# A vision tower's last stage on one core: scores, maximum and exponential run one tile further ahead of the transposes, with two probability buffers, ScalarE copying the attention output out of PSUM, and three gather buffers in place of four

## The reference

```python
# B=4, SEQ=2048, D=64, HEADS=8, KEYS=64, TOPK=16
x    = layernorm(h)
sim  = scores of x against two sets of 64 product keys     # per token, per head
rows = the 16 best of the 64 x 64 key pairs                # top-k of the sums
w    = softmax(the 16 best sums)
k, v = sum over the 16 rows of w * table[row]              # 128 values a token
q    = x @ Wq / 8
p    = softmax(causal(q @ k.T))                            # 2048 x 2048, masked
h   += (p @ v) @ Wo
```

## Time and profile before

| | |
|---|---|
| median of 3 runs | 13776.14 us (13771.75 to 13789.44) |
| profiled execution, first to last instruction | 17300.9 us; no other time of it is given |
| instructions | 137100 |
| TensorE matmuls busy | 10525.5 us (61%) |
| VectorE busy | 9604.5 us (56%) |
| ScalarE busy | 6663.5 us (39%) |
| GpSimd busy | 6947.2 us (40%) |

### The profile page before, as it was taken

The page is one execution under the profiler, slowest core; times in us unless marked ns, Lnnn a source line. Parts: engine busy times, 40 slices in busy tenths (PEclk is TensorE's granted clock), DMA queues, the critical chain, the costliest instruction groups (busy, mean ns, idle before and its releaser), DMA issues.

```text
span 17300.9 us, 137100 instructions
## 1 busy us (share of the span) xinstructions
PE 10525.5 (61%) x38012; PEld 5367.1 (31%) x38012; DVE 9604.5 (56%) x22115; ACT 6663.5 (39%) x13997; POOL 6947.2 (40%) x5868
## 2 busy tenths in 40 slices
PE   1564555554655366666666666666666666666667
PEld 1341222222212123333333333333333333333334
DVE  3327888887675654555544555455554454555542
ACT  0113333341002144444444444444444444444443
POOL 2004666764000254444444444444444444444442
PEclk9556777776677577877787778787877777777776
DMA  0001222221000111111111111111111111111110
GB/s 20 0 13 69 90 105 102 107 89 69 12 11 5 31 40 38 35 41 35 40 34 38 37 38 38 35 38 37 38 35 41 33 41 34 38 38 37 38 35 20
DMA packets 538556, 722.95 MB, mean 42 GB/s; under 512 B 412866, under 2 KB 420593, under 8 KB 503386
## 3 DMA queue, kind: packets, MB, share of 16 engines
q0 software_dynamic: 168448, 338.54, 7.4%
q1 hardware_dynamic: 369418, 376.55, 7.1%
HBM read 697.87 MB, written 8.42 MB: 41 GB/s over the span
## 4 chain that ended last, share of the span: by engine, by line
PE 25%; another core or an unknown queue 16%; ACT 14%; issue 7%; DVE 3%; DVEq 1%; ACTq 0%
ACT l3m_spread L2479 5%; PE l3m_O L2353 5%; PE l3m_acc L2385 4%; PE l3m_DX L2375 4%; PE l3m_S L2336 3%; ACT l3m_V L2521 2%; PE l3m_T L2343 2%; ACT l3m_prob L2508 2%; PE l3m_S L2375 2%; ACT l3m_W L2525 2%; ACT l3m_probT L2517 1%; PE l3m_DX L2376 1%; PE l3m_T L2296 1%; PE l3m_T L2321 1%
## 5 line engine op out<-in xcount | busy, mean ns | idle before, releaser
L2278 POOL DMA_INDIRECT l3m_got<-in_l_table,l3m_row x5120 | 4995.9, 976 | 6236.5 <-ACT l3m_spread L2479 3620.8
L2385 PE MATMUL l3m_acc<-l3m_W,l3m_values 128*128 128x512 f32 x3072 | 2014.8, 743 | 922.9 <-issue 512.8
L2734 DVE SCALAR_TENSOR_TENSOR tower_h<-l3m_O,l3m_pinv,tower_h 128x64 f32<-128x64 f32 x512 | 145.4, 284 | 3520.3 <-PE l3m_O L2353 2621.6
L2479 ACT ACTIVATE l3m_spread<-l3m_got,l3m_weight 128x128 f32<-128x128 f32 x5120 | 1924.1, 493 | 12.4 <-issue 12.4
L2517 ACT ACTIVATE l3m_probT<-l3m_T 128x512 f32<-128x512 f32 (+3 forms) x1280 | 679.8, 531 | 1756.8 <-remote 1108.3
L2353 PE MATMUL l3m_O<-l3m_vo_g,l3m_probT 128*128 128x64 f32 x5440 | 861.0, 306 | 678.5 <-ACT l3m_probT L2517 459.5
L1262 POOL TENSOR_TENSOR m_mul<-m_st,m_wide_c 128x2048 f32<-128x2048 f32 x256 | 1157.5, 4521 | 149.9 <-DVE m_st L1415 143.7
L2353 PEld LDWEIGHTS l3m_O<-l3m_vo_g,l3m_probT 128*128 128x128 f32 x5440 | 832.3, 222 | 916.2 <-ACT l3m_probT L2517 570.5
L2525 ACT ACTIVATE l3m_W<-l3m_DX 128x512 f32<-128x512 f32 x971 | 579.3, 597 | 1258.9 <-PE l3m_DX L2376 563.2
L2343 PE MATMUL l3m_T<-tower_ident,l3m_prob 128*128 128x128 f32 x4352 | 844.9, 317 | 286.9 <-issue 160.2
L2385 PEld LDWEIGHTS l3m_acc<-l3m_W,l3m_values 128*128 128x128 f32 x3072 | 592.9, 223 | 1301.5 <-issue 684.5
(11 more groups left out here) (689 smaller groups left out, 21609.8 us busy)
## 6 DMA issues: line engine op xcount, KB each, us to landing
m_wide_c<-l1a_c SPq DMA_DIRECT2D x256, 1024.0 KB, 4.6
l3m_got<-in_l_table,l3m_row POOLq DMA_INDIRECT x5120
l3m_values<-in_l_table SPq DMA_DIRECT2D x288, 256.0 KB
l0i_img<-in_l_x SPq DMA_DIRECT2D x4, 1024.0 KB, 7.9
l2r_x<-l2a_hT SPq DMA_DIRECT2D x8, 512.0 KB, 5.5
qp_inw<-in_q_inw SPq DMA_DIRECT2D x1, 2336.0 KB, 7.8
l_kept<-l0t_xt,l0t_row POOLq DMA_INDIRECT x128
l1a_c<-m_mul SPq DMA_DIRECT2D x16, 128.0 KB, 2.6
```

Source lines behind the costliest of these rows:

```text
L2278: pool.indirect_dma_start(got[:, unit % GOT, j, :], None, table, bass.IndirectOffsetOnAxis(ap=row[:, unit // QUAD % RING, unit % QUAD, j:j ...
L2385: pe.matmul(acc[:], values[:, tile, :], W[:], start=(tile == 0), stop=(tile == TILES - 1)).then_inc(blended, 1)
L2479: copy = act.activation(spread[:, unit % 2, :, j], got[:, unit % GOT, j, :], ACT.Copy, scale=weight[:, g % RING, t, j:j + 1])
```

## The change

TensorE's `scores` moves from the start of a step to its end and takes the tile after the next: at the end of step s it scores tile n + 2. VectorE's `peak` takes tile n + 1 in step s, and ScalarE's `attend` takes tile n + 1 in the middle of step s (behind turn `turns // 2`, and ahead of the `lift` of the next turn). For that `prob` has two buffers. `O` keeps one region of 64 columns; a new ScalarE copy `take_mix` at the start of each step brings tile n - 1's output to `mixes` (four slots), and `scale` reads it there one step later than before. The extras q, kv and vo are made three tiles ahead in place of two, `GOT` falls from 4 to 3, and there is one step more.

```diff
-STEPS = QUAD * (QUADS + LAG) + 1
+STEPS = QUAD * (QUADS + LAG) + 2
-GOT, RING = 4, 5
+GOT, RING = 3, 5
+SLOTS, AHEAD = 4, 3
...
     def made_at(s):
-        n = tile_at(s + 2)
+        n = tile_at(s + AHEAD)
...
     def wide(s):
-        return any(n is not None and depth[n] >= 3 * QUAD for n in (tile_at(s), tile_at(s + 1)))
+        return any(n is not None and depth[n] >= 3 * QUAD for n in (tile_at(s + 1), tile_at(s + 2)))
...
-        prob, probT = u.sb("prob", [P, SEQ]), u.sb("probT", [P, 2, CH])
-        nmax, psum, pinv = u.sb("nmax", [P, 2]), u.sb("psum", [P, 2]), u.sb("pinv", [P, 2])
+        prob, probT = u.sb("prob", [P, 2, SEQ]), u.sb("probT", [P, 2, CH])
+        nmax, psum, pinv = u.sb("nmax", [P, 2]), u.sb("psum", [P, SLOTS]), u.sb("pinv", [P, 2])
+        mixes = u.sb("mixes", [P, SLOTS, D])
...
             def mixing(n, c):
                 if n >= 1 and c == 0:
-                    pe.wait_ge(scaled, n)
+                    pe.wait_ge(o_taken, n)
...
-                    last = pe.matmul(O[:, n % 2 * D:(n % 2 + 1) * D],
+                    last = pe.matmul(O[:, 0:D],
...
             for s in range(STEPS):
-                n, nxt = tile_at(s), tile_at(s + 1)
+                n, later = tile_at(s), tile_at(s + 2)
                 todo = pieces(s)
                 if todo:
                     onward(todo[0])
                 elif pieces(s - 1):
                     blend(TILES * DQ - 1)
-                if nxt is not None:
-                    scores(nxt, max((k + 1 for k in second if k < first_piece(s)), default=0))
...
                     if c + 1 < len(todo):
                         onward(todo[c + 1])
+                if later is not None:
+                    scores(later, max((k + 1 for k in second if k < first_piece(s + 1)), default=0))
...
             def attend(n):
                 act.wait_ge(peaked, n + 1)
-                if n >= 2:
-                    act.wait_ge(scaled, n - 1)
+                if n >= SLOTS:
+                    act.wait_ge(scaled, n - SLOTS + 1)
...
+            def take_mix(n):
+                act.wait_ge(mixed, chunk0[n + 1])
+                if n >= SLOTS:
+                    act.wait_ge(scaled, n - SLOTS + 1)
+                act.activation(mixes[:, n % SLOTS, :], O[:, 0:D], ACT.Copy).then_inc(o_taken, 1)
...
-                if n is not None:
-                    attend(n)
+                coming, middle = tile_at(s + 1), turns(s) // 2
+                if tile_at(s - 1) is not None:
+                    take_mix(tile_at(s - 1))
                 if todo:
                     lift(todo[0])
                 part_up(mine[0:share])
+                if coming is not None and turns(s) == 0:
+                    attend(coming)
...
                     part_up(mine[(c + 1) * share:(c + 2) * share])
+                    if c == middle and coming is not None:
+                        attend(coming)
                     if c + 1 < len(todo):
                         lift(todo[c + 1])
...
             def scale(n):
-                dve.wait_ge(mixed, chunk0[n + 1])
-                dve.scalar_tensor_tensor(h[:, at, :], O[:, n % 2 * D:(n % 2 + 1) * D], pinv[:, n % 2:n % 2 + 1],
+                dve.wait_ge(o_taken, n + 1)
+                dve.scalar_tensor_tensor(h[:, at, :], mixes[:, n % SLOTS, :], pinv[:, n % 2:n % 2 + 1],
...
             for s in range(STEPS):
-                n = tile_at(s)
+                coming = tile_at(s + 1)
...
-                if n is not None:
-                    peak(n)
+                if coming is not None:
+                    peak(coming)
...
-                before = tile_at(s - 1)
+                before = tile_at(s - 2)
```

More of the change, by code:

```diff
@@ L2229, in mix_heads @@
         grown, blended = u.sem("grown"), u.sem("blended")
-        staged, placed = u.sem("staged"), u.sem("placed")
+        staged, placed, o_taken = u.sem("staged"), u.sem("placed"), u.sem("o_taken")
         tabled = [u.sem(f"tabled{i}") for i in range(4)]
@@ L2342, in flip @@
                 for a in range(4 * c, min(4 * c + 4, depth[n] + 1)):
-                    last = pe.transpose(T[:, (a % 4) * P:(a % 4 + 1) * P], prob[:, a * P:(a + 1) * P], ident[:])
+                    last = pe.transpose(T[:, (a % 4) * P:(a % 4 + 1) * P], prob[:, n % 2, a * P:(a + 1) * P], ident[:])
                 last.then_inc(t_made, 1)
@@ L2504, in attend @@
                 act.wait_ge(peaked, n + 1)
-                if n >= 2:
-                    act.wait_ge(scaled, n - 1)
+                if n >= SLOTS:
+                    act.wait_ge(scaled, n - SLOTS + 1)
                 to = (depth[n] + 1) * P
-                act.activation(prob[:, 0:to], S[:, 0:to], ACT.Exp,
-                               bias=nmax[:, n % 2:n % 2 + 1], accum_out=psum[:, n % 2:n % 2 + 1]).then_inc(expd, 1)
+                act.activation(prob[:, n % 2, 0:to], S[:, 0:to], ACT.Exp, bias=nmax[:, n % 2:n % 2 + 1],
+                               accum_out=psum[:, n % SLOTS:n % SLOTS + 1]).then_inc(expd, 1)
+            def take_mix(n):
[3 more added lines that the diff above has]
+                act.activation(mixes[:, n % SLOTS, :], O[:, 0:D], ACT.Copy).then_inc(o_taken, 1)
             def take_flip(n, c):
@@ L2583, in _ @@
                     for use in extras(s)[c:c + 1]:
-                        take_extra(use, (s + 2 - QUAD * LAG) // QUAD % 2)
+                        take_extra(use, (s + AHEAD - QUAD * LAG) // QUAD % 2)
                     part_up(mine[(c + 1) * share:(c + 2) * share])
+                    if c == middle and coming is not None:
+                        attend(coming)
                     if c + 1 < len(todo):
@@ L2730, in scale @@
                 dve.wait_ge(expd, n + 1)
-                dve.reciprocal(pinv[:, n % 2:n % 2 + 1], psum[:, n % 2:n % 2 + 1])
+                dve.reciprocal(pinv[:, n % 2:n % 2 + 1], psum[:, n % SLOTS:n % SLOTS + 1])
                 dve.drain()
-                dve.wait_ge(mixed, chunk0[n + 1])
-                dve.scalar_tensor_tensor(h[:, at, :], O[:, n % 2 * D:(n % 2 + 1) * D], pinv[:, n % 2:n % 2 + 1],
+                dve.wait_ge(o_taken, n + 1)
+                dve.scalar_tensor_tensor(h[:, at, :], mixes[:, n % SLOTS, :], pinv[:, n % 2:n % 2 + 1],
                                          h[:, at, :], ALU.mult, ALU.add).then_inc(scaled, 1)
```

## The result

| | us | ratio to the kernel before, 95% interval |
|---|---|---|
| kernel before | 13782.79 (13771.75 to 13795.24, 4 runs) | |
| changed kernel | 13968.24 (13954.56 to 13984.24, 4 runs) | 1.0137 [1.0122, 1.0151] |

The change makes the kernel 185 us slower; 13990 was forecast, with slower at 0.58.

The account below looks back on a forecast made before the run. TensorE was taken to set the pace, with 0.9 to 3.2 us of idle time a step, nearly all waiting for ScalarE. The terms sum to +215 us on 13776, given as 13990 us, range 13500 to 14330.

Parts of the forecast that it names:

- wait for the exponential at the seam, and VectorE's late maxima: Start of a step: TensorE's scores stop waiting for the exponential, -350 us; ScalarE stops waiting for VectorE's maximum, -90.
- exponential in its new place: Middle of a step: the exponential delays the next V or last probT, 90% of its 589 us exposed, +530 us.
- start of a step without cover: First mixing waits for ScalarE without scores to cover it, 1.0 us in 26% of steps, 0.1 elsewhere: +170 us.
- blend's wait for W: At the seam: the wait goes, as the scores now stand between, 0.15 us a step, -75 us.
- `take_mix`: 512 new 64-column ScalarE copies at the step start, estimated 0.20 us each, covered by TensorE's scores: 0 us.
- extras, now three tiles ahead and in one step: q, kv and vo fall with ranks and centred; 26 steps get extra turns of some 1.2 us: +30 us.
- three gather buffers: GpSimd's gathers: it needs 20 us for a tile's issues and may start 47 us ahead: 0 us.
- What bounds the kernel: TensorE sets the pace, waiting nearly only for ScalarE; the profile's extra 3525 us are stops that timed runs mostly lack.
- VectorE idling at the mask-add in place of scale changes nothing: Start of VectorE's step: waiting there for scores, not at `scale` for the last mixing, was taken to cost nothing.
- The middle hides the exponential: Rival, middle of a step: less than 315 of 589 us exposed makes it faster, about 13600 us; chance 0.27.
- Nothing is won at the seam: Rival: the seam's wait turns up again as waits for V or probT, +655 us, 14430 us; chance 0.09.
- The clock: Rival: less idle time raises the stage's clock from 0.79 to 0.85, 500 us less, 13280 us; chance 0.05.

Follow-up runs that it names:

- e0: The kernel before, unchanged, profiled again for a trace without the stops of the first profile: 13809.14 us in one run, span 13807.4.
- e7: The changed kernel with q, kv and vo made two tiles ahead again in place of three: 14292.90 us, ratio 1.0379 to the kernel before.
- e4: The kernel before with three gather buffers in place of four and nothing else: 13770.92 us, ratio 0.9995.
- e8: The changed kernel with the edits of e5 and e6 together, on a chip where the kernel before takes 17571.99 us: 17396.90 us, ratio 0.9891.
- e1: The changed kernel with ScalarE's next lift (V) ahead of the exponential in the middle of a step: 13816.44 us, ratio 1.0023 to the kernel before.
- e5: The changed kernel with the exponential moved into the last turn, between probT and W: 13678.74 us, ratio 0.9928 to the kernel before.
- e6: The changed kernel with the level ahead of the blend at every seam: 13886.48 us, ratio 1.0083 to the kernel before.
- e9: e8 with VectorE's mask and maximum moved behind its picking (`top_pairs`), on the same chip as e8: 17360.26 us, ratio 0.9861 to the kernel before.
- e2: The changed kernel plus four 4-column ScalarE copies behind the exponential in the middle of each step: 14251.42 us, ratio 1.0338 to the kernel before.
- e3: The changed kernel plus the same four copies as e2, but behind `take_mix` at the seam: 14011.67 us, ratio 1.0163 to the kernel before.

## Why the prediction was right, point by point

The forecast was +215 us, the result +185. Terms by the waits at their positions, e0 against after:

| step of the prediction | forecast | measured |
|---|---|---|
| wait for the exponential at the seam, and VectorE's late maxima | -350 - 90 | -514 (520.4 to 6.8; 200.5 of it was ScalarE waiting for the maximum) |
| exponential in its new place | +530 | +472 (V3 +319, T4 +153); 74 of V3's stand behind copies that stopped for a sum |
| start of a step without cover | +170 | +189 (V1 +84, T1 +105) |
| blend's wait for W | -75 | -113 |
| `take_mix` | 0 | 0 (226 ns each, at an idle place) |
| extras, now three tiles ahead and in one step | +30 | +92 (kv 60.8, ranks 31.4; both are gone in e7); extra turns not singled out |
| three gather buffers | 0 | 0 (e4) |

The measured waits add to +126, where the sum has +215; the spans differ by 156 and the timed medians by 185. What is not waiting isn't singled out; beside it stands the granted clock, 0.95 before and 0.94 after. The terms miss by -74, -58, +19, -38 and +62 us and partly cancel, so the direction and the order of the terms are earned, and a forecast within 30 us of the result is in part luck.

- *What bounds the kernel.* Right in the main: TensorE sets the pace, its idle time is for ScalarE, and the step length in microseconds held (14.7 us in the working, 15.0 in e0, where the 512 tiles take 7701). The reading that the 3525 us were stops which the timed runs lack held for the timed runs that it was made for; the chip of e8 has such stops in timed runs too. Because of them V, probT and W looked too large and the exponential too small.
- *The exponential in the middle.* Mechanism and place as forecast: e1 takes 318 us at V3 away and leaves T4, e5 takes both away. The size is 472 of 589 us, 80% exposed, and the sum had 90%, from a single step with 0.05 us of slack. Not all of the 472 is the exponential: V3's waits behind stopped copies grew from 60 to 134 us. The Trainium skill ("Perfetto Trace Analysis", Optimizing Scalar/DVE Operations) says that breaking up the instructions of such an engine may let work end sooner. The waits agree as to the bubble that moves; no run here breaks the exponential up, and e5 shows that another place does it with the exponential whole.
- *Start of a step.* The term was a count, 26% of steps by 1.0 us and the rest by 0.1, and came out within 20 us, but not with its parts: the working gave 133 us to the steps where the blend stands ahead of the level, and e6, which turns them round, takes 94 us of V1 and T1 away; the rest stays. The first mixing of a four-chunk step waits 0.37 us on average where it waits, not 1.
- *The seam.* Two terms, -350 and -90, measured -514 together. ScalarE waited 200.5 us for the maximum, in the step's first place. If all of that was TensorE's wait too, which isn't shown, the two are some 310 and 200: the first about as forecast, the second too small by 110, as 71.0 us in the trace with stops had stood for it. Together the bounds, 281 to 679, held it.
- *`take_mix`.* The row is below; its idle time of 75.4 us is ScalarE waiting for the last mixing, at a place where it then waits for the level anyway, as the 2.75 us above show. By the Trainium skill ("VectorE: DVE Perf Modes", the section on the TRN2 errata) a copy is an estimated 0.20 us; measured are 0.226 on average, from 0.198 to 0.268.

```profile
L2517 ACT ACTIVATE l3m_mixes<-l3m_O 128x64 f32<-128x64 f32 x512 | 115.9, 226 | 75.4 <-PE l3m_O L2355 75.4
```

- *The rivals.* "The middle hides the exponential" needed less than 315 of 589 us exposed; there were 472. "Nothing is won at the seam" is out, as the seam's wait went and the time stayed far below 14430. The clock moved the other way from the rival, by a hundredth.
- *What failed.* "VectorE idling at the mask-add in place of scale changes nothing" didn't hold. Both stand at the start of VectorE's step, ahead of the picking, but `scale` waited for the last mixing and the mask-add now waits for the scores behind it. The sums come later: the copies' idle time rises by 72 us and V3's waits behind it by 74. The idle time alone doesn't tell the loss: in e5, the fastest kernel on this chip, the copies idle 184.1 us. And the extras: their pile-up was counted as a cost of 30 us, and costs at least the 92 us of late kv and ranks, but making them two tiles ahead again in e7 lost 325 us, as the sums came later still. The sum has no term for that.

Open: why the sums are later in e7 than in the changed kernel; whether the late maximum (e9) helps on a chip without stops; and e8 on such a chip, where e5 alone gives 0.9928.

## What to carry to other kernels

Before moving a long instruction on an in-order engine, look at what stands right behind it and who waits for that, and at what the engine idles for at the place that it leaves: the same exponential cost 472 us ahead of a V or the last probT, and some 149 in the last turn. The half-busy ScalarE had no free time where it hands pieces back and forth with TensorE: work added there cost 283 us for 195, and at the seam 43. When a stop has no name in the profile, look which instruction ended just before it did: here it was a sum, not the weights that the code waits for first. And profile the kernel before on a chip whose span agrees with the timed runs before ranking its waits.

## What the runs showed of the hardware

- One program (the kernel before), two chips: 13779.17 and 17571.99 us. On the latter, e8 has 18% of its chain on an unknown queue; on the former, the changed kernel has 1%.
- The granted clock of the stage differed with the same matmuls: 0.95 before, 0.94 after, 0.92 with e2's copies, and TensorE was busy 125 us longer in e2 than in e3. It doesn't simply follow the waits: in the rows for the exponential, V, W and probT e5 waits 291 us less than e0, and it has 0.838 over the whole program, e0 0.845.
- Small activations overlap: four of 128x4 took 0.48 us together, and the next instruction began 0.38 us after the first.
- A 128x64 copy out of PSUM on ScalarE took 226 ns.
